# Three units of a set turned in blocks as one group; attends in three visits; SyncE's order of a set's transfers changed

## What is computed

```python
q = (x @ Wq + bq).reshape(n, H, C)          # k, v alike
attn = einsum('nhc,mhc->hnm', q, k) / sqrt(C)
neg = where(adj == 0, -inf, attn)
e = where(adj == 0, 0, exp(neg - max(neg)))
out = einsum('hnm,mhc->hnc', e / sum(e), v)
beta = sigmoid(concat([out, x_r, out - x_r]) @ Wb);  y = beta * x_r + (1 - beta) * out
```

## Time and profile before

| | |
|---|---|
| median of 3 runs (all) | 1783.71 us (1783.48, 1783.71, 1785.61) |
| the profiled execution, its own time | 1785.83 us |
| its span | 1784.2 us |
| attention stage, about | 575 to 1542 us |
| granted PE clock, mean | 0.992 |

### The profile page before, as it was taken

One profiled execution on the slowest core, in us unless ns is written; L12 is line 12 of the kernel. 1 busy time (PEld: TensorE's weight loads), 2 busy tenths in 40 slices (PEclk: granted clock), 3 DMA queues, 4 the chain that ended last, 5 costly groups with the idle time before them and its releaser, 6 DMA issues.

```text
span 1784.2 us, 40293 instructions
## 1 busy us (share of the span) xinstructions
PE 1738.6 (97%) x15000; PEld 1132.1 (63%) x15000; DVE 1228.7 (69%) x2405; ACT 975.8 (55%) x1505; POOL 895.6 (50%) x849
## 2 busy tenths in 40 slices
PE   7999999999998999999999999999999999999996
PEld 3444444444444778887877877778778777644442
DVE  4777775222125889999999999999999999301322
ACT  0110111010002898999999999999999999411101
POOL 0211111111114755778878788788787896540211
PEclk9999999999999999999999999999999999999998
DMA  9866766789996644545445455454454543797991
GB/s 374 308 224 245 256 253 246 258 308 371 341 359 192 195 143 164 160 149 165 149 149 173 143 165 161 162 167 156 142 180 143 163 162 117 313 372 273 326 322 62
DMA packets 134029, 388.53 MB, mean 218 GB/s; under 512 B 15712, under 2 KB 66144, under 8 KB 109280
## 3 DMA queue, kind: packets, MB, share of 16 engines
q1 hardware_dynamic: 116928, 355.78, 57.5%
q10 hardware_dynamic: 14688, 23.08, 3.6%
q0 software_dynamic: 2240, 7.34, 1.6%
HBM read 333.19 MB, written 52.95 MB: 216 GB/s over the span
## 4 chain that ended last, share of the span: by engine, by line
PE 91%; DVE 4%; issue 1%; DMA 1%; ACT 1%; POOL 1%; SPq 1%; DVEq 0%; ACTq 0%; POOLq 0%
PE bank L588 34%; PE bank L739 23%; PE bank L760 14%; PE bank L698 13%; DVE arena L1278 2%; PE bank L576 1%; DMA arena<-adj_cols 1%; PE bank L651 1%; PE bank L610 1%; PE bank L609 1%; PE bank L603 0%; PE bank L766 0%; PE bank L646 0%; PE bank L786 0%; PE bank L626 0%
## 5 line engine op out<-in xcount | busy, mean ns | idle before, releaser
L973 ACT ACTIVATE arena<-arena,small 128x2048 f32<-128x2048 f32 x256 | 516.1, 2016 | 2.8 <-DVE small L1278 2.8
L739 PE MATMUL bank<-ident,arena 128*128 128x128 f32 x3592 | 485.5, 278 | 4.3 <-ACT arena L973 2.6
L739 PEld LDWEIGHTS bank<-ident,arena 128*128 128x128 f32 x3592 | 398.1, 141 | 87.7 <-issue 42.1
L588 PE MATMUL bank<-arena,stat_s 128*128 128x512 f32 x1008 | 439.1, 593 | 2.1 <-issue 1.2
L985 ACT ACTIVATE arena<-bank 128x512 f32<-128x512 f32 x673 | 377.1, 604 | 66.3 <-PE bank L739 65.6
L698 PE MATMUL bank<-k,parts 128*128 128x512 f32 x1024 | 354.4, 436 | 10.7 <-DVE small L1278 10.7
L588 PEld LDWEIGHTS bank<-arena,stat_s 128*128 128x128 f32 x1008 | 189.3, 190 | 226.8 <-issue 225.3
L760 PE MATMUL bank<-arena,stat_x 128*32 128x128 f32 x8192 | 276.5, 276 | 0.0
L760 PEld LDWEIGHTS bank<-arena,stat_x 128*32 128x32 f32 x8192 | 208.1, 109 | 90.8 <-issue 81.6
L588 PE MATMUL bank<-arena,stat_x 128*128 128x512 f32 x512 | 230.9, 602 | 10.8 <-DMA arena<-adj_cols 8.5
L698 PEld LDWEIGHTS bank<-k,parts 128*128 128x128 f32 x1024 | 158.8, 192 | 29.6 <-DVE small L1278 24.6
(11 more groups left out here) (155 smaller groups left out, 1432.1 us busy)
## 6 DMA issues: line engine op xcount, KB each, us to landing
arena<-adj_cols SPq DMA_DIRECT2D x190, 1024.0 KB, 6.2
stat_s<-adj SPq DMA_DIRECT2D x85, 512.0 KB, 4.7
group_dram<-stat_s SPq DMA_DIRECT2D x63, 512.0 KB, 2.9
arena<-group_dram SPq DMA_DIRECT2D x252, 128.0 KB, 2.8
arena<-adj SPq DMA_DIRECT2D x43, 512.0 KB, 4.7
parts<-q_dram SPq DMA_DIRECT2D x128, 64.0 KB, 2.4
k<-k_dram POOLq DMA_DIRECT2D x28, 256.0 KB, 9.3
x_dram<-arena ACTq DMA_DIRECT2D x16, 256.0 KB, 3.6
```

The lines of the kernel that those rows point to most:

```text
L588: mm_ = pe.matmul(bank[:, to, :], stat[:, jt, :], ring[:, s, j, :], start=(jt == 0), stop=(jt == TILES - 1))
L739: last = pe.transpose(bank[:, b_, h * P:(h + 1) * P], cols[:, st % SETS, h, u * P:(u + 1) * P], ident[:, :])
L973: act.activation(cols[:, s_, h, :], cols[:, s_, h, :], ACT.Exp, bias=shift[:, t % 2, 1, i:i + 1], scale=-1.0, accum_out=blocksum[:, t % 2, ...
```

## The change

Units 13, 14 and 15 of a set are turned in blocks, at places 1, 2 and 6, stored as one transfer of 768 KB and read by four of 192 KB. The PE-turned units of a set are 13; they take the eight `turned` slots in turn by their order among PE units. The group gets slots of its own, in `stat_s`. PE attends at place 4 (the last four units of the set before), at place 8 (units 0 to 5) and at place 14 (units 6 to 11). The adjacency has two buffers, loads go out 7 biases ahead, and six chunks of xt (0 to 5) are spilled; PE waits for all six before layer 3's first matmul. SP's order per set: store of the group, (xt store), mask load, load of the group, mask load, queries. Copies by DVE are 23 of a chunk's 104, by ACT 81. Exponents are at other places, and so are two late steps of the chunk's end (logs 119 to 121, norm_h 113 to 115).

```diff
-ATTEND_BATCH = 4
-ATTEND_LAG = 8
-BLOCK_TURN_AT = {14: 3, 15: 5}
-GROUPS = ((14, 15),)
-VECTOR_PLACES = (6,)
+ATTENDS = {4: (-4, -3, -2, -1), 8: (0, 1, 2, 3, 4, 5), 14: (6, 7, 8, 9, 10, 11)}
+BLOCK_TURN_AT = {13: 1, 14: 2, 15: 6}
+GROUPS = ((13, 14, 15),)
+VECTOR_PLACES = ()
+VECTOR_ALSO = (5, 6, 7, 19, 25, 27, 38, 54, 58, 59, 66, 69, 82, 86, 87, 91, 92, 97, 99, 103, 119, 121, 123)
...
-MASK_AHEAD = 8
-MASKS = 3
-SPILLED = (2, 3, 4, 5)
+MASK_AHEAD = 7
+MASKS = 2
+SPILLED = (0, 1, 2, 3, 4, 5)
...
+def slot_of(k):
+
+    return (PE_UNITS + LAST_UNITS).index(k) % TURNED
...
+def used_before(c, k):
+
+    i = (PE_UNITS + LAST_UNITS).index(k) - TURNED
+    return c * UPC + PE_UNITS[i] + 1 if i >= 0 else (c - 1) * UPC + PE_UNITS[i] + 1
...
-        group_slots = arena[:, RING + 10 * CHUNK:RING + 12 * CHUNK]
...
-        adj_in = (arena[:, RING + 4 * CHUNK:RING + 6 * CHUNK], spilled[:, 0:2 * CHUNK], spilled[:, 2 * CHUNK:4 * CHUNK])
...
+        adj_in = (arena[:, RING + 4 * CHUNK:RING + 6 * CHUNK], spilled[:, 0:2 * CHUNK])
+        group_slots = spilled[:, 2 * CHUNK:5 * CHUNK]
+        blocks = [stat_s[:, TILES - 3 * TPC:TILES, :].rearrange("p t f -> p (t f)")]
...
-                if g * UPS + GROUPS[i][-1] >= TURNED:
-                    sp.wait_ge(unit_used, g * UPS + GROUPS[i][-1] - TURNED + 1)
+                if g > 0:
+                    sp.wait_ge(unit_used, (g - 1) * UPS + GROUPS[i][-1] + 1)
...
                     g = c * SPC + st
-                    load_mask_ahead(c, 2 * st + 0)
                     if g < GROUP_SETS:
                         store_group(g, 0)
                     if st == 0 and c - 2 in SPILLED:
                         store_xt(c - 2)
+                    load_mask_ahead(c, 2 * st - 1 if g == 0 else 2 * st)
                     if g < GROUP_SETS:
                         load_group(g, 0)
+                    if g == 0:
+                        load_mask_ahead(c, 2 * st)
+                    load_mask_ahead(c, 2 * st + 1)
                     if st % SETS == 0:
                         ahead = c * TPC + st // SETS + 2
                         if ahead < CHUNKS * TPC:
                             load_queries(ahead // TPC, ahead % TPC, False)
-                    load_mask_ahead(c, 2 * st + 1)
...
+                sp.wait_ge(unit_used, GROUP_SETS * UPS)
                 for i in range(len(SPILLED)):
...
-                    if (k - ATTEND_LAG) % ATTEND_BATCH == 0:
-                        for a in range(k - ATTEND_LAG, k - ATTEND_LAG + ATTEND_BATCH):
-                            if a >= 0:
-                                attend(c, a, first)
-                            elif not first:
-                                attend(c - 1, UPC + a, False)
+                    for a in attended_at(c, k):
+                        if a >= 0:
+                            attend(c, a, first)
+                        elif not first:
+                            attend(c - 1, UPC + a, False)
...
-            product(2, 0, {0: [final_out], SPILLED[0] - 1: [lambda: pe.wait_ge(xt_in_place, 16 * len(SPILLED))], 5: [lambda: pe.wait_ge(att_pool, AG(last - 1, "xt"))],
+            pe.wait_ge(xt_in_place, 16 * len(SPILLED))
+            product(2, 0, {0: [final_out], 5: [lambda: pe.wait_ge(att_pool, AG(last - 1, "xt"))],
```

More of the change, by code:

```diff
@@ L198, in last_bank_before, with attended_at @@
     return TURN_BANKS.uses[LAST_USE + 1 + LAST_UNITS.index(k) - len(TURN_BANKS.BANKS)][1]
+def attended_at(c, k):
+    u = k % UPS
+    return [k - u + a for a in ATTENDS.get(u, ())]
+def slot_of(k):
[3 more added lines that the diff above has]
+    return c * UPC + PE_UNITS[i] + 1 if i >= 0 else (c - 1) * UPC + PE_UNITS[i] + 1
 BY_VECTOR = [k for k in PE_UNITS if (k % 16 in VECTOR_PLACES or k in VECTOR_ALSO) and k not in VECTOR_NOT]
@@ L287, in build_program @@
         cols = arena[:, 0:RING].rearrange("p (s h n) -> p s h n", s=2, h=H)
+        spilled = stat_s[:, SPILLED[0] * TPC:(SPILLED[-1] + 1) * TPC, :].rearrange("p t f -> p (t f)")
         turned = [stages[i] for i in (0, 1, 6, 7, 2, 3, 10, 11)]
[L289 to L293 removed]
+        adj_in = (arena[:, RING + 4 * CHUNK:RING + 6 * CHUNK], spilled[:, 0:2 * CHUNK])
+        group_slots = spilled[:, 2 * CHUNK:5 * CHUNK]
+        blocks = [stat_s[:, TILES - 3 * TPC:TILES, :].rearrange("p t f -> p (t f)")]
         maskbias = [half_[:, i * BLOCK:(i + 1) * BLOCK] for half_ in
@@ L305, in slots_of @@
         def slots_of(i):
-            first, n = GROUPS[i][0] % TURNED - 6, len(GROUPS[i])
-            return group_slots[:, first * CHUNK:(first + n) * CHUNK]
+            return group_slots[:, 0:len(GROUPS[i]) * CHUNK]
         def tiles(ap):
@@ L537, in _ @@
                              q_parts[:, i, :].bitcast(F32)).then_inc(gcn_q_out, 16)
-            load_mask(0, 5)
+            load_mask(0, 4)
             sp.wait_ge(gcn_dve, CV(last, "root"))
             sp.dma_start(root_dram[:, last * CHUNK:CHUNKS * CHUNK], root_out).then_inc(gcn_root_out, 16)
-            for m in range(6, MASK_AHEAD):
+            for m in range(5, MASK_AHEAD - 1):
                 load_mask(0, m)
@@ L758, in attend @@
                     else:
-                        weights = turned[k % TURNED][:, h * P:(h + 1) * P]
+                        weights = turned[slot_of(k)][:, h * P:(h + 1) * P]
                     last = pe.matmul(to, stat_x[:, k % UPT, h * C:(h + 1) * C], weights,
@@ L812, in attention @@
                 if last_chunk:
-                    for a in range(UPC - ATTEND_LAG, UPC):
+                    for a in range(UPC - 4, UPC):
                         attend(c, a, first)
@@ L978, in copy_unit @@
                 if not (first and k < TURNED):
[L979 to L985, removed]
+                    act.wait_ge(unit_used, used_before(c, k))
+                elif k >= TURNED - 2:
+                    act.wait_ge(gcn_x2_out, 16 * CHUNKS)
+                elif k >= TURNED - 4:
+                    act.wait_ge(gcn_k_out, 32 * CHUNKS)
+                act.activation(turned[slot_of(k)], bank[:, unit_bank(k), :],
                                ACT.Copy).then_inc(unit_copied_act, 1)
@@ L1046, in attention @@
                         block_weights(c, k // UPT)
-                    if k in BY_SCALAR or (last_chunk and k == LAST_UNITS[1]):
+                    if k in BY_SCALAR or (last_chunk and k in LAST_BY_SCALAR):
                         copy_unit(c, k, first)
@@ L1374, in attention @@
             def attention(c, first, last_chunk):
-                post = post_steps(c - 1, 107 if last_chunk else 113) if not first else {}
+                post = post_steps(c - 1, 107 if last_chunk else 115) if not first else {}
                 for k in range(UPC):
@@ L1394, in attention @@
                             turn_blocks(c, k - place + u)
-                    if k in BY_VECTOR or (last_chunk and k == LAST_UNITS[0]):
+                    if k in BY_VECTOR or (last_chunk and k in LAST_BY_VECTOR):
                         copy_unit(c, k, first)
```

37 lines of the change are left out of this document (17 added, 20 removed).

## The result

The changed kernel takes **1814.21 us** (median of 6 runs, 1812.72 to 1815.34) against 1785.32 for the kernel before (6 runs): ratio 1.0161, 95% interval 1.0151 to 1.0171. It is 28.9 us slower, where 17 us less was forecast and 1783 was the upper end of the range.

What follows compares the result with a forecast made beforehand. PE was taken to bound the kernel before, DVE after the change. Sets -23.6, start +1 and end +5 made -17.6 us: 1785.83 to 1768.2, by the median of runs 1766.1, given as 1767; range 1755 to 1783.

Steps and rivals of the forecast that it cites:

- The engines' part: Floors per set: PE 14.33 us, DVE 14.35, ACT 13.79; with waits a set takes 14.60, in all -23.6 us.
- DVE becomes the longest: Per set, block turn for 5/8 of a copy adds 0.25 us to DVE: floor 14.35, above PE's 14.33.
- the forecast's 0.38: Each of 62 sets takes 14.60 us, 0.38 us less than before: -23.6 us.
- Masks ... Cost 0 (bound: 1 us x 7 chunks): Adjacency loads into two buffers: POOL waits many times, DVE never for a bias; only ACT's logs have little slack.
- The group's way ... Cost 0: Group's store and loads through DRAM: 9.0 us from the store's issue, hidden until place 4, 2.7 us to spare.
- Rival C: Group arrives after place 4 once its way exceeds 11.7 us; PE waits every set; about 1797 to 1828 us; chance 0.10.
- The end: Before layer 3's first matmul PE waits for six xt loads behind ring loads: +5 us (bounds 0 and 6).
- The start: In the first set, paced by DVE, block turns stand earlier and are one more: +1 us.
- the price of a visit: PE's three attend visits a set for four: 0.22 us saved a set, bounds 0.13 (exit alone) and 0.31.

Runs made afterwards that it cites:

- e10_after_no_masks: The changed kernel with the attention's adjacency loads left out but for the first two, masked by wrong rows: 1783.79 us (10 runs), ratio 0.9989 to the kernel before.

## Why the prediction was wrong

**The engines' part came out in one chunk, and there in part by luck.** Chunk 1 of `e10_after_no_masks`, then chunk 1 of the kernel before, columns as in the earlier trace rows:

```profile
713.88:830.57 116.69, 114.71 (x1591) 93.55 (x1589) 113.38 (x211) 110.66 (x164) 91.78 (x85) 1.00 0.44 126
```

```profile
712.53:831.94 119.41, 119.20 (x1623) 95.81 (x1621) 112.26 (x208) 112.12 (x167) 93.30 (x89) 1.00 0.48 155
```

By eighths PE is busy 14.34 us a set (its floor was put at 14.33), ACT 13.83 (13.79), but DVE 14.17 and not 14.35. Its block turn for 5/8 of a copy costs 0.14 us a set from one chunk 1 to the other, not 0.25. So "DVE becomes the longest" is wrong: PE still is. The set of 14.59 came out because PE's floor lies where DVE's was put, and PE is idle the 0.25 that was meant for DVE; DVE is idle 0.41. The number is right in that step, the engine is not. An estimate by the figures of the Trainium skill ("VectorE: DVE Perf Modes", the TRN2 errata) was +0.18 a set and a floor of 14.28, below PE's. The trace agrees with that order, and 0.18 is nearer to the measured 0.14 than the 0.25 from the rows. Block turns are 189 and transposes 3340 on the page.

The forecast also took every chunk to be alike. Chunks 2 to 6 of that kernel take 118.9 us in the mean where they took 119.9, so 0.12 us a set is left there of the forecast's 0.38.

**The step that failed is "Masks ... Cost 0 (bound: 1 us x 7 chunks)".** It said rightly that POOL would stand for adjacency many times, and that DVE would not wait for a bias. It had the first load of a set right, but the second goes out 7.0 us after the group's store in the median (5.8 to 8.3), about place 14 and not 11, for it stands behind the group's loads, which wait for the store to land. Between a load's landing and the bias made from it lie 2.0 us in the median of chunks 1 to 6, where 8.5 lay before. The step then asked who else waits for POOL and named ACT's logs alone. Two others hang on the same queue of POOL: the blend, which DVE's statistics need in the third set, and xt, which SP needs in the first. It priced POOL's standing by the slack of the result that POOL waits *with* (the bias, over 8 us), and not by that of the results queued *behind* it. Those had little: with no mask waited for, DVE still stands for the blend in each chunk from 2 on. The earlier trace rows already pointed there: POOL is busy 82.73 of 100 us, a number that the prediction passed over, and with 103 us of standing in 900 that comes to 94 by an estimate, as full as DVE was. What the runs put in the place of 0 is 27.4 us.

**"The group's way ... Cost 0" failed with it**, in the size of its loads. The store lands in 4.1 us in the median (4.4 taken), the loads in 3.9, and 8.4 at most (2.8 taken, 4.8 the bound). In seven sets of eight the whole way is 9.1 to 11.7 us, not 9.0. In the first set of chunks 2 to 7 it is 12.6 to 13.9. The working counted SP's mask load between store and loads but not `store_xt`, which the diff puts there, and which now waits for POOL. That wait holds the loads up by 0.8 to 1.1 us in chunks 5 to 7, and not at all in chunks 2 to 4. The rest is the loads themselves: from the first one's issue to the last one's landing they take 7.7 to 9.7 us there, beside mask and query loads, and 5.4 to 6.5 in the same sets of the kernel without masks. Most of it goes when POOL is on time, though the masks are still loaded: PE's wait in the first sets is then 4.7 us in all and not 14.0. So POOL's lateness is the root, and C is one of the two ways in which that reached PE.

**Rival C had the right side and place**, and a tenth of the chances. Its threshold of 11.7 us was too high: PE's wait in the first sets is the way less 10.9 to 11.0 us, in part because these sets take 14.2 us and not 14.6. It lacked its cause, and so took every set to be alike, where it fell on one set of eight. It also had the lost microseconds at face value, where the lower clock behind some of the stands adds to them.

**The end was sized at +5 and is 7.5.** The wait was 5.23, so the step held; the eight matmuls behind it, 1.9 us longer at the lower clock, were not in it. **The start** was +1 and is -0.3 (first store and chunk 0).

**The sum as it stands**, in medians and with the causes taken away in this order: 1814.21, less 27.4 for POOL's waits for masks, 1.5 for SP's, 1.6 for their bytes, 1.5 for xt, 7.6 for the order at the end, is 1774.7. It is 7.7 above the forecast. Chunks 2 to 6 alone are 9.6 above it (118.5, 118.8, 118.8, 118.6, 118.9 against 116.8), so the other terms together were 2 too high. That POOL's own work makes these chunks longer is read from a timeline and not shown: no kernel with fewer POOL steps was tried.

**What stays open:** the price of a visit, since both runs that changed the visits also broke the tables written for them (an estimate: PE is busy 0.56 us a set less from one chunk 1 to the other, and 0.43 of it is the unit, which leaves 0.13, the lower bound given); and whether three adjacency buffers would let this change win, as the memory for a third went to the group's slots. The runs without mask loads say what it might be: level with the kernel before as it stands (0.9989), and 0.55% faster with the wait for xt gone and the end's order put right.

## What to carry to other kernels

When a change makes an in-order engine stand, list everything queued behind the wait on that engine and everyone who waits for each of those results, not only for the result the wait is about. A buffer taken away is paid either by the queue that loads it or by the engine that reads it; a change of order chooses which, and the cost is that of what is queued behind. A helper's mean of 50% busy says little of its slack: read it in the stretch where it has the most to do (POOL was at 83% there), and add what the change makes it wait. When a number comes out, look whether the engine that was to set it is the one that did.

## What was unexpected in the hardware

PE's clock. In 965 to 970 us PE was busy 2.34 of 5 us at a granted clock of 0.99; in 970 to 975, behind a single stand of 3.02 us, the granted clock was 0.67, a mean over time at 1.2 and time at 2.4 GHz. Attends and transposes took 1.51 and 1.80 us there for 0.86 and 1.03, 1.4 us more. Behind the stand of 5.23 us at the end it was 0.66 in 1570 to 1576 us, and eight matmuls took 5.57 us for 3.67, 1.9 more. So these two stands cost a third to a half more than their own length.

The length of a stand does not tell by itself. Two others of the same kernel, in chunks 6 and 7 (timeline of PE):

```profile
1338.01 1.07 PE L776 MATMUL bank<-stat_s,stat_x 128*32 128x128 f32 x24 [1.84 <-DMA stat_s<-group_dram]
```

```profile
1463.02 0.86 PE L776 MATMUL bank<-stat_s,stat_x 128*32 128x128 f32 x24 [2.93 <-DMA stat_s<-group_dram]
```

Behind the one of 1.84 us the granted clock is 0.72 over 1337.5 to 1343.5 us; around the one of 2.93 us (1462.5 to 1468.5) it stays at 1.00, and the attends take 0.86 us as ever. What decides between them no run here shows.

The Trainium skill ("TensorE: Matmul & The Clock Gate", Part 1) puts an idle array at 1.2 GHz and a busy one at 2.4; the granted clocks of 0.67 and 0.66 behind the stands of 3.02 and 5.23 us agree with that.
